# Second expert layer's gate weights: two fp32r parts and one product per block, instead of three bf16 parts and two products

## The reference, cut to what matters

```python
probs = softmax(xf @ router_w + router_b)
tw, ti = top_k(probs, 8)
tw = tw / sum(tw)
# for each expert e of 64
h  = silu(xf @ W1[e] + B1[e]) @ W2[e] + B2[e]
cw = sum(where(ti == e, tw, 0.0), axis=-1)
acc = acc + cw[:, None] * h
# and the shared experts, unweighted
out = routed + sum over shared of silu(xf @ W1 + B1) @ W2 + B2
```

## Time and profile before

| | |
|---|---|
| three timed runs | 1447.47, 1448.64, 1450.95 us, median 1448.64 |
| the profiled execution's own time | 1445.63 us |
| its span, first to last instruction | 1443.8 us |
| mean granted TensorE clock | 0.892 of full |
| TensorE matmul busy | 1135.5 us, 79% |
| VectorE busy | 981.0 us, 68% |
| ScalarE busy | 720.4 us, 50% |
| GpSimd busy | 615.1 us, 43% |

### The profile page before, as it was taken

One profiled execution on the slowest core, in us unless ns is written; L12 is line 12 of the kernel. 1 busy time (PEld: TensorE's weight loads), 2 busy tenths in 40 slices (PEclk: granted clock), 3 DMA queues, 4 the chain that ended last, 5 costly groups with the idle time before them and its releaser, 6 DMA issues.

```text
span 1443.8 us, 13324 instructions
## 1 busy us (share of the span) xinstructions
PE 1135.5 (79%) x3910; PEld 570.5 (40%) x3922; DVE 981.0 (68%) x2194; ACT 720.4 (50%) x1376; POOL 615.1 (43%) x426
## 2 busy tenths in 40 slices
PE   4225968877887969678787876968997899999797
PEld 1002323333332323333333533535453465556565
DVE  5965787578866887467657797555645545549787
ACT  7506653476437552442524524435563357756564
POOL 1970787148732965122113574453423122224322
PEclk7557979988899979689898999989998999999898
DMA  6000000000000000200001000000000200000000
GB/s 209 0 0 1 0 1 0 1 0 1 0 1 1 1 0 0 101 0 1 0 1 66 1 1 1 1 1 1 1 1 0 66 0 1 8 1 8 0 9 7
DMA packets 11271, 17.76 MB, mean 12 GB/s; under 512 B 1304, under 2 KB 7584, under 8 KB 10688
## 3 DMA queue, kind: packets, MB, share of 16 engines
q1 hardware_dynamic: 11200, 16.93, 3.5%
HBM read 15.88 MB, written 1.05 MB: 12 GB/s over the span
## 4 chain that ended last, share of the span: by engine, by line
PE 39%; DVE 12%; ACT 5%; issue 3%; POOL 2%; POOLq 0%; DVEq 0%; ACTq 0%
PE bankE L1840 6%; PE bankE L1225 3%; PE bankS L1803 2%; PE bankE L1757 2%; PE bankS L1788 2%; PE bankS L1757 2%; PE bankE L1287 2%; PE bankE L620 1%; PE bankS L1760 1%; PE bankE L1246 1%; PE bankE L1760 1%; PE bankS L1730 1%; PE bankE L579 1%; PE bankE L1275 1%; PE bankE L613 1%
## 5 line engine op out<-in xcount | busy, mean ns | idle before, releaser
L732 DVE TENSOR_TENSOR_SCAN hs<-dA,carry,bankS 128x512 f32<-128x512 f32 x128 | 156.7, 1266 | 3.1
L332 POOL TENSOR_TENSOR hc<-hs,cb 128x1024 f32<-128x1024 f32 x56 | 131.8, 2353 | 46.3 <-DVE hs L732 43.4
L307 POOL TENSOR_TENSOR cv<-cv,hc 128x1024 f32<-128x1024 f32 x56 | 132.6, 2368 | 4.4
L1715 ACT ACTIVATE c_h<-bankE,C 128x512 f32<-128x512 f32 x144 | 98.7, 687 | 53.1 <-PE bankE L1840 50.7
L1609 POOL TENSOR_TENSOR c_acc<-c_acc,c_tw 128x512 f32<-128x512 f32 x32 | 45.9, 1434 | 159.6 <-DVE c_tw L1934 159.5
L443 ACT ACTIVATE sg<-bankE,C 128x512 f32<-128x512 f32 x80 | 54.8, 687 | 97.2 <-PE bankE L579 96.9
L724 DVE TENSOR_TENSOR bankS<-dx,bankS 128x1024 f32<-128x1024 f32 x64 | 78.3, 1224 | 6.5 <-PE bankS L508 5.9
L1840 PE MATMUL bankE<-c_fH,c_w1H 128*128 128x512 f32 x144 | 81.3, 565 | 1.1 <-ACT c_h L1715 1.1
L393 ACT ACTIVATE dA<-dl,Aneg 128x512 f32<-128x512 f32 x128 | 80.2, 708 | 0.1
L508 PE MATMUL bankS<-bc,sel 96*128 96x512 bf16 x60 | 28.0, 466 | 59.6 <-DVE hs L732 59.6
L542 PE MATMUL bankE<-h2T,wg 128*128 128x512 f32 x128 | 71.2, 639 | 4.0 <-ACT sg L424 1.9
(11 more groups left out here) (523 smaller groups left out, 2899.8 us busy)
## 6 DMA issues: line engine op xcount, KB each, us to landing
c_w<-in_w SPq DMA_DIRECT2D x1, 2304.0 KB, 8.7
X<-in_x SPq DMA_DIRECT2D x4, 256.0 KB, 3.9
wg<-in_gate_T SPq DMA_DIRECT2D x1, 1024.0 KB, 8.0
wu<-in_up_T SPq DMA_DIRECT2D x1, 1024.0 KB, 10.2
f<-in_w SPq DMA_DIRECT2D x1, 1024.0 KB, 7.1
out<-X SPq DMA_DIRECT2D x4, 256.0 KB, 2.3
b_wq<-in_Wqkv SPq DMA_DIRECT2D x1, 768.0 KB, 4.5
g<-in_sw SPq DMA_DIRECT2D x2, 256.0 KB, 3.5
```

The source lines that it names most:

```text
L307: pool.tensor_tensor(cv[:, :, :], cv[:, :, :], (hv if by_vector(i, k) else hc)[:, :, :], ALU.add).then_inc(s["y_acc"], 1)
L332: pool.tensor_tensor(dst[:, :, :], hs[:, k % HS, :, :], cb[:, k % 2, :].unsqueeze(1).to_broadcast([P, HV, G]), ALU.mult).then_inc(s["hc_re ...
L732: V.tensor_tensor_scan(hs[:, k % HS, h, :], dA[:, (HV * k + q) % DA, :], dbx[:, h, :], carry[:, k, h:h + 1], ALU.mult, ALU.add).then_inc(s ...
L1715: act.activation(h[:, n % 3, :], E[k % 2][:, :], ACT.Gelu_apprx_tanh, bias=col("b1_3", k)).then_inc(s["fs_ready"], 1)
```

## The change

The weights are kept in two fp32r parts: the rounded weight and the rest. Both stand in `c12`, on 128 rows. `c3` is gone, and the second of the two products per block with it. In the split, ScalarE's two roundings of the rest and VectorE's second subtraction go; VectorE's one subtraction now writes the lower half of `c12` itself and sets `w3_ready`. `selE` becomes fp32r as well. The layer before (piece `R4`) keeps its three bf16 parts; only its semaphore counts change, since `R6` no longer adds to them. `selE` needs more memory (4 bytes instead of 2 per entry); the room comes from a reserve at the low end of SBUF that the builder kept for DMA descriptors, halved from 16384 to 8192 bytes, so everything is laid out 8192 bytes lower.

```diff
-MAMBA_END = 134112
-KL_END = 124512
-WINDOW_END = 192192
+MAMBA_END = 125920
+KL_END = 116320
+WINDOW_END = 184000
...
-    self_ = sb2("selE", [P, EB1, 4, H1], BF16)
+    self_ = sb2("selE", [P, EB1, 4, H1], F32R)
...
-    wrr = sb2("wrr", [E1N, G])
-    wtt = sb2("wtt", [E1N, G], BF16)
+    wrr = sb2("wrr", [8, G])
+    wtt = sb2("wtt", [8, G], BF16)
     cwT = sb2("cwT", [E1N, G])
-    c12 = sb2("c12", [P, G], BF16)
-    c3 = sb2("c3", [E1N, G], BF16)
+    c12 = sb2("c12", [P, G], F32R)
...
                 act.activation(cwT[:, :], E[3][0:E1N, :], ACT.Copy).then_inc(s["w_high"], 1)
-                at_least(act, s["w_rest"], e, 2, 2)
-                act.activation(wtt[:, :], wrr[:, :], ACT.Copy).then_inc(s["w_mid"], 1)
-                act.activation(c12[E1N:2 * E1N, :], wrr[:, :], ACT.Copy).then_inc(s["w_mid"], 1)
...
-                    pe.matmul(EC[b % 2][:, :], self_[:, b, :, :].rearrange("p a b -> p (a b)"), c12[:, :], start=True, stop=False)
-                    pe.matmul(EC[b % 2][:, :], self_[0:E1N, b, :, :].rearrange("p a b -> p (a b)"), c3[:, :], start=False, stop=True).then_inc(s["cw_ready"], 1)
+                    pe.matmul(EC[b % 2][:, :], self_[:, b, :, :].rearrange("p a b -> p (a b)"), c12[:, :], start=True, stop=True).then_inc(s["cw_ready"], 1)
...
                 at_least(V, s["w_high"], e, 3, 3)
-                V.tensor_tensor(wrr[:, :], E[3][0:E1N, :], c12[0:E1N, :], ALU.subtract).then_inc(s["w_rest"], 1)
-                at_least(V, s["w_mid"], e, 4, 4)
-                V.tensor_tensor(c3[:, :], wrr[:, :], wtt[:, :], ALU.subtract).then_inc(s["w3_ready"], 1)
+                V.tensor_tensor(c12[E1N:2 * E1N, :], E[3][0:E1N, :], c12[0:E1N, :].bitcast(F32), ALU.subtract).then_inc(s["w3_ready"], 1)
...
-SBUF = (16512, 229368)
+SBUF = (8320, 229368)
+SCRATCH = 8192
...
-    nc = bacc.Bacc("TRN2", target_bir_lowering=False, num_devices=1)
+    nc = bacc.Bacc("TRN2", target_bir_lowering=False, num_devices=1, dynamic_dma_scratch_size=SCRATCH)
```

More of the change, by code:

```diff
@@ L407, in piece @@
                 act.activation(w3[0:8, :], E[3][0:8, :], ACT.Copy).then_inc(s["w_high"], 1)
-                at_least(act, s["w_rest"], e, 2, 1)
+                at_least(act, s["w_rest"], e, 1, 1)
                 act.activation(wtt[0:8, :], wrr[0:8, :], ACT.Copy).then_inc(s["w_mid"], 1)
@@ L783, in piece @@
                 V.tensor_tensor(wrr[0:8, :], E[3][0:8, :], w3[0:8, :], ALU.subtract).then_inc(s["w_rest"], 1)
-                at_least(V, s["w_mid"], e, 4, 2)
+                at_least(V, s["w_mid"], e, 2, 2)
                 V.tensor_tensor(w3[64:72, :], wrr[0:8, :], wtt[0:8, :], ALU.subtract).then_inc(s["w3_ready"], 1)
```

## The result

| | before | changed |
|---|---|---|
| timed runs, median | 1448.41 us (4 runs, 1447.47 to 1450.95) | 1427.97 us (4 runs, 1426.70 to 1430.71) |
| profiled execution, its span | 1445.63, 1443.8 us | 1427.41, 1425.6 us |
| mean granted TensorE clock | 0.892 | 0.889 |
| TensorE matmul busy | 1135.5 us | 1116.5 us |
| VectorE busy | 981.0 us | 977.8 us |

The changed kernel is faster: ratio 0.9864, 95% interval 0.9847 to 0.9881. Timed once more beside other kernels it took 1426.03 us, ratio 0.9841 (0.9825 to 0.9857). Forecast were 1426 us and 1416 to 1437.

The account below looks back on a forecast made before the run. Gated steps were taken as bound by the ring cw, hh, down product, next cw; split 8.4, steps 12.6 and clock 1.2 sum to 22.2 us, taking the median 1448.6 to 1426 us, range 1416 to 1437.

Parts of the forecast that it names:

- The bound: Bare gated steps: the ring cw (spread of gate weights), hh, down product, next cw sets the step, 2.50 us falling to 2.19.
- rival 2: Gated steps: TensorE's stream alone sets the step, going toward 1.95 us; 7.0 us more gain, time 1419; chance 0.09.
- The steps: The 60 gated steps behind the four first ones: 12.6 us gained, 9.0 of it from 29 bare steps at 0.31.
- the three steps put at 0.40: Gated steps with another product ahead of L465 or L478: 0.40 us gained each, 1.2 in all.
- five steps with another product between in group four: Gated steps ahead of L1152 (3 at 0.46 us) and of L1170 and L1179 (2 at 0.50): 2.4 us.
- What would show it: Signs in the new trace: steps 2.19 us, scan rounds 5.13, about 0.6 behind the subtraction, TensorE busy down some 20 or more.
- The split: Weight split ahead of each group: first hh earlier by 2.4, 2.8, 1.5 and 1.7 us in groups one to four, 8.4 summed.
- The clock: Behind group one's split: without TensorE's idle time the half-clock stretch goes, 1.2 us gained; chance falls plus or minus 3 us.
- the forecast's own range: Whole kernel: 1421 to 1432 us, with 3 for the clock, 1 for memory, 0.4 at each split, some steps miscounted.
- Rival 3: Gated steps: more TensorE idling drops the clock to 1.2 GHz, 1.7 us more per such step, time 1462; chance 0.05.
- The memory: selE written as fp32r, SBUF 8 KB lower with half the descriptor reserve: 0 us, 1 us to either side.

Follow-up runs that it names:

- spread_first: The changed kernel with the spread product issued ahead of the previous step's down product, from the second gated step on; 1431.33 us, ratio 0.9882.
- bf16_single: The changed kernel with selE and c12 in bf16 instead of fp32r, the third part of the weights left out; 1429.34 us, ratio 0.9867.
- memory_only: The kernel before with everything laid 8192 bytes lower and the descriptor reserve halved, nothing else; 1449.65 us, ratio 1.0003.
- steps_only: The changed kernel with the old split's two roundings, second subtraction and waits back, the single fp32r product kept; 1439.45 us, ratio 0.9941.
- rows_128: The kernel before with the second spread product on all 128 rows too, the lower half zero; 1445.10 us, ratio 0.9965.
- split_only: The kernel before with the new one-subtraction split alone, both bf16 products kept and part three zero; 1440.64 us, ratio 0.9942.
- after_again: The changed kernel, unedited, profiled and timed once more; 1426.03 us, ratio 0.9841.

## Why the prediction was right

**The bound.** Right. The ring cw, `hh`, down product, next cw sets the bare steps; spread_first opened it, and the step fell to TensorE's stream, 1.95, the number worked out for rival 2. In the changed kernel the step is 2.19, so rival 2 falls: the hand-over of 1.02 didn't shrink with the emptier queue.

**The steps.** Mechanism right, size 11.2 against 12.6. The bare ones measured 0.30 to 0.31 for 0.31 forecast, 31 for 29 counted. What was too high is the rest: the three steps put at 0.40 don't show as a class of their own (group two has a single 0.09), and of five steps with another product between in group four three show (0.45, 0.50, 0.45). The split of the 0.31 in columns (0.22) and change of rows (0.09) was tested by itself: 0.21 and 0.10.

**What would show it.** The step, the round of 5.13 and the 0.6 behind the subtraction came as written. TensorE's busy time fell by 19.0, not 20 or more. "The spread product 0.40 long, `hh` 0.48 after its start" was wrong for the record and right for the work: the fp32r record behind an f32 product is 0.80 long, and its columns are read as starting about 0.4 behind its start.

**The split.** The sum of 8.4 came out, and in part by luck: 1.5 of clock too much in group three stands against 1.1 too little in group four. Groups one and two: 2.14 and 2.55 for 2.4 and 2.8, a little too high, for L719 itself starts the `hh` 1.24 later, where 1.1 was taken. Group three: 1.5 forecast and 1.46 from the split (1.47 in bf16_single); the other 1.50 of the 2.96 is a vanished half-clock stretch that was in no term. Group four: 1.7 forecast, 0.71 measured. What failed is that TensorE's work at the split runs as fast as before. L618 at 687.36 took 1.91 where its partner took 1.28, and 0.64 of the lead goes there; 0.46 more goes ahead of the split, where the lead falls from 13.48 to 13.02 while products of 0.27 take 0.42. The wait of 0.87 for `sg` is gone, as forecast. Without the clock the 0.71 would be about 1.8, an estimate from these rows; the split alone in group four remains untested at full clock.

**The clock.** The term of 1.2 came out at 1.27: the stretch at 226.4 did go and gave 0.96 and 0.31. Its cause is borne out in part. Of the ten profiles, the four with the old split each have one short half-clock stretch directly behind TensorE's idle time at the split of group one or two, the kernel before and memory_only in group one, steps_only and rows_128 in group two; the six with the new split have none at either place. So the idle time looks needed for the stretch, but it doesn't bring it by itself: behind the same idle time group two of before and group one of steps_only and rows_128 run at full clock. Why one group and not the other is open. A second stretch, at 264, gave 1.49 that was in no term; it is still there in split_only, steps_only and memory_only and gone in rows_128, so neither half of the change took it away by itself. Other stretches came: at the start 1.65 (chance, by after_again), between groups 0.46 and 2.07. Over the span the half-clock time was 313 us before and 317 after. The 3 us to either side in the forecast's own range was about the right size for a median; for one profile it is small, as one stretch alone cost 4.15.

Why is the time 20.4 us lower by the medians (24.6 in the second set) and the span only 18.2? The profiled execution of before was one of its quickest: 1445.63, where the 36 timed runs of it lay at 1445.95 to 1452.46, and its mean clock was 0.892, where the runs of 1452.11 and 1452.46 us had 0.885 and 0.886. (One of 1452.04 us had 0.889, so the mean clock doesn't tell it all.) These runs have no trace, but memory_only's profile of 1451.58 us shows what such a run can hold: its part of this layer runs like before's to 0.02 us an `hh`, and it is 2.5 slower ahead of group one and 4.15 slower in the later layer. That the slower runs of before held these stretches is likely, not shown.

**Rival 3.** Falls. The gated steps of group one, each shorter of a product, ran at a granted 1.00 throughout (window of the changed kernel, busy of PE, PEld, DVE, ACT, POOL, clock):

```profile
228.00:280.00 52.00, 44.33 (x117) 18.24 (x116) 37.36 (x85) 20.30 (x30) 24.25 (x13) 1.00 0.00 1
```

That is 85% busy at 2.4 GHz, like the stretch of the earlier trace rows. **The memory** is zero, as put.

**Open.** Why the 13.7 us at half clock between groups three and four became 23.9. It did so in every other run but memory_only (each lost 1.9 to 2.0 at the first `hh` of group four; in spread_first the half clock lasted 41 us). So neither the split nor the single product brings it by itself; the kernels that have it share only that their work lies otherwise against the half-clock stretches than in the profile of before.

## What to carry to other kernels

Price a removed product at a gated step by the ring that the step waits on, not by the engine's busy time: 64 products of 0.39 us went, and of the 60 steps behind the first ones 31 gained 0.3, three 0.45 or 0.5, and the other 26 little or nothing. Ask of two products in a row whether their rows differ: 64 rows behind 128 cost 0.10 more than 128 behind 128, each way. Before opening a ring, count what the next engine needs for a round; here GpSimd's 4.95 lay just below the 5.13, and opening the ring made the timed runs no faster. And where half-clock stretches come and go, read a gain at its own place in the trace: a stretch that vanished ahead of the split doubled its gain in group three.

## What the runs showed of the hardware that I had not expected

- Filling the second product's 64 rows up to 128 with zeros made the kernel faster, ratio 0.9965 (0.9953 to 0.9977): a bare step takes 2.39 instead of 2.50, since the product's weight load then lies under the product ahead. The steps are some 3 us of it.
- The fp32r product in a step costs the same as bf16 to 0.01 us (2.19 and 2.18).
- The first 117 us can differ by 1.5 us between two executions of one program (1.27 behind before and 0.26 ahead of it at the first `hh`), and half-clock stretches far from any edit come and go, worth 1 to 2 us each and one of them 4.15. Two profiles can't tell an edit of 2 us in this kernel; the steps, read one by one, tell one of 0.1.
